# Scores of two heads, then the part of an expert, then the scores of the other two heads

## The chip, the cores and the metric

The kernel runs on one core of a Trainium2 chip. The metric is the device time of one execution in microseconds (us), as a median over runs. The core has five engines that work from their own instruction queues and meet through semaphores: TensorE (PE in the profile, its weight loads PEld), VectorE (DVE), ScalarE (ACT), GpSimd (POOL) and SyncE (SP, which issues most transfers). SBUF is the working memory. PSUM, with eight banks of 128 x 512 f32, is where TensorE writes.

## The reference, cut to what matters

One layer over 2048 tokens of 128 features. First an attention with 16 heads of 8 features, in which a sigmoid stands where a softmax would be; then a mixture of experts: each token goes to two of eight experts, and a shared expert sees every token.

```python
align = jnp.einsum('bhtd,bhsd->bhts', q, k)
resonance = jax.nn.sigmoid((align - THRESH) * SHARP)
modulation = resonance * gate_q[..., :, None] * gate_k[..., None, :]
collapse = jnp.einsum('bhts,bhsd->bhtd', modulation, v)
...
out = out + comb[:, e:e + 1] * _swiglu(xn, gate_up_w[e], down_w[e])   # for the two experts of a token
out = out + _swiglu(xn, shared_gate_up_w, shared_down_w)
```

## The kernel before

The tokens are cut into four blocks of 512 (`TB`). Attention of block `i` is done in 64 rounds `k` (`ROUNDS`): four groups of four heads (`g = k // 16`), and for each group 16 tiles of 128 keys (`s = k % 16`). In a round TensorE computes the scores of four heads against one key tile (`scores`), ACT puts the sigmoid over them (`sigmoids`), and TensorE multiplies the result by the gated values and adds it up in the bank `AV` (`values`). `values` runs one round late: round `k` does the scores of `k` and the values of `k - 1`.

The scores of a round are two halves of two heads. A head has 32 contracted rows, head `j` of the group on partitions `32 j` to `32 j + 31`, so its matmul uses a quarter of the array's rows, and the four matmuls of a round use four different quarters. A half goes to a pair of PSUM banks, and one ACTIVATE of 128 x 1024 takes it. There are three such pairs (`S[0:2]`, `S[2:4]`, `UO`), used in turn: half `n` may be written when the sigmoid of half `n - 3` is done (`scores_before`). With two halves a round, the first half of round `k` waits for the second sigmoid of round `k - 2`, and the second half for the first sigmoid of round `k - 1`. After each half a semaphore (`score_mm`) tells ACT.

The experts of the block before are computed in the gaps of the same rounds. `NT` = 15 tiles of 128 rows sorted by expert, and the shared expert, make 16 units `u`. Each unit has three kinds of part: part 0 is the gate projection (`gate`, 12 matmuls, for the shared expert 3), part 2 the up projection (`up`, as many), and part 1 the down projection of unit `u - 3` (`hidden_out`, 12 matmuls) with the turning of a tile (`turn_tile`, 2 matmuls). All parts, and the projections of the attention, share one bank (`GB`). So each waits for the engine that reads what was there before (the list `readers`): mostly DVE, which clips the gate, multiplies gate by up, or copies the output. Which round has which part is fixed by `parts_in`: rounds 22 to 60 have one each, rounds 17, 20 and 21 have the shared expert's, and in blocks 2 and 3 rounds 10 and 12 to 19 carry the last nine parts of the block before. Rounds of `i` = 0 have no parts, and behind round 63 of `i` = 3 comes a last stage without attention. Within the three blocks, `i` = 1 has 42 rounds with a part, `i` = 2 and 3 have 50 each: 142 together.

The order on TensorE in a round is written out by hand in `rounds`: the scores, the steps of the routing (`project_last`, `turn_tokens`, `route`, `rank`, only in rounds 1, 8, 9 and 11), the first part, the values of the round before, and then whatever else the round has (a second part, `gate_rows`). Steps of the end of a block (`finish`) run on DVE in rounds 36 to 41 of blocks 2 and 3.

Of the kernel before, what the change touches and what calls it, by code (L numbers as in the profile page):

```python
# [27 lines left out]
G = 4  # L28
# [72 lines left out]
def scores_before(n):  # L101

    return max([m + 1 for m in range(max(n - 40, 0), n) if score_pair(m) == score_pair(n)], default=0)
# [6 lines left out]
def parts_in(i, k):  # L110

    parts = [(i - 1, *CARRIED_PARTS[n])
             for n, at in enumerate(CARRIED) if at == k and i > 1]
    parts += [(i, 0, part) for part, at in SHARED_PARTS.items() if at == k]
    if FIRST_PART <= k <= LAST_PART:
        parts.append((i, *PARTS[k - FIRST_PART]))
    return parts if i > 0 else []


def build(nc, x, wqkv, vecs, consts, ident16, wo, router, gu, down, out):  # L120
    ctx = ExitStack()
    with ctx:  # L122
# [110 lines left out]
        heads = [m[:, :, 0:2 * D].rearrange("p s (n d) -> p s n d", d=HD) for m in raw]  # L233
# [119 lines left out]
        def turned_with(u):  # L353

            return (0, 1) if u == 0 else tuple(range(u + 1, min(u + 2, NT)))
# [12 lines left out]
        def score_banks(i, k, half):  # L368

            pair = score_pair(2 * (i * ROUNDS + k) + half)  # L370
            return UO[:] if pair == 2 else S[:, 2 * pair:2 * pair + 2, :]
# [44 lines left out]
        def wait(eng, s, value):  # L416

            if not isinstance(value, int) or value > 0:
                eng.wait_ge(s, value)
# [323 lines left out]
        def _(pe):  # L743
# [48 lines left out]
                                split[:, n // 2, first:first + G, :, :].rearrange("p n s d -> p (n s d)"), id16[:, K_IDENT:K_IDENT + P])  # L792
                    mm.then_inc(qk_tr, 1)

            def scores(i, k):
                g, s = k // ST, k % ST
                if i == 0:
                    pe.wait_ge(qk_copied, 4 * (s // SUB + 1))
                elif s == 0:
                    pe.wait_ge(q_staged[g], i * 16)  # L800
                for j in range(G):
                    if j % 2 == 0:

                        wait(pe, sig_done, scores_before(2 * (i * ROUNDS + k) + j // 2))
                        if (i, k, j) == (0, WIDE_FROM, 0):

                            pe.wait_ge(qk_copied, 4 * NB)
                        banks = score_banks(i, k, j // 2)
                    r = slice(32 * j, 32 * j + 32)
                    mm = nc.tensor.matmul(banks[:, j % 2, :], kT[r, g, s * P:(s + 1) * P], qT[r, g, :], start=True, stop=True)  # L810
                    if j % 2 == 1:
                        mm.then_inc(score_mm, 1)
# [35 lines left out]
            def project_last(i):  # L848

                pe.wait_ge(coll_ready, i * NG)  # L850
                for j in range(SUB):
                    mm = nc.tensor.matmul(GB[:, j * D:(j + 1) * D], coll[:, NG - 1, j * P:(j + 1) * P], wo_sb[:, NG - 1, :],
                                          start=False, stop=j == SUB - 1)
                mm.then_inc(proj_mm, 1)

            def turn_tokens(i):
                pe.wait_ge(n2_ready, i)
                for j in range(SUB):
                    mm = nc.tensor.transpose(GB[:, j * P:(j + 1) * P], tok[:, j, :], ident)
                mm.then_inc(n2_mm, 1)  # L860

            def route(i):

                pe.wait_ge(xn_ready, i * 3 - 2)
                for j in range(SUB):
                    mm = nc.tensor.matmul(GB[:, j * E:(j + 1) * E], xnT[:, j * P:(j + 1) * P], rws[:], start=True, stop=True)
                mm.then_inc(router_mm, 1)
# [6 lines left out]
            def rank(i, readers):  # L874

                free(readers)
                pe.wait_ge(mask_ready, i)
                under, ones = id16[:, K_UNDER:K_UNDER + P], id16[:, K_ONES:K_ONES + P]
                for j in range(SUB):
                    for m in range(j + 1):  # L880
                        nc.tensor.matmul(GB[:, j * E:(j + 1) * E], under if m == j else ones, mask[:, m, :], start=m == 0, stop=m == j)
                for m in range(SUB):
                    mm = nc.tensor.matmul(GB[:, SUB * E:(SUB + 1) * E], ones, mask[:, m, :], start=m == 0, stop=m == SUB - 1)
                mm.then_inc(rank_mm, 1)
# [28 lines left out]
            def gate(i, u, readers):  # L913

                n, m = (i - 1) * NU + u, (i - 1) * NT + u - 1
                free(readers)
                if u == 0:
                    pe.wait_ge(xn_ready, i * 3)
                    pe.wait_ge(weights_split, E + 1)
                else:  # L920
                    pe.wait_ge(tile_turned, m + 1)
                    pe.wait_ge(gu_loaded[m % GS], (m // GS + 1) * 16)
                expand(gate_bank(i, u), u, m, 0).then_inc(gate_mm, 1)
                return [(gate_clipped, n + 1)]

            def up(i, u, readers):

                n, m = (i - 1) * NU + u, (i - 1) * NT + u - 1
                free(readers)
                expand(up_bank(i, u), u, m, 1).then_inc(up_mm, 1)  # L930
                return [(prod_ready, n + 1)]
# [13 lines left out]
            def hidden_out(i, u, readers):  # L945

                n, m = (i - 1) * NU + u, (i - 1) * NT + u - 1
                free(readers)
                pe.wait_ge(hid_split, n + 1)
                pe.wait_ge(dn_loaded[m % DS], (m // DS + 1) * 16)  # L950
                w = dn_ring[:, m % DS, :].rearrange("p (h c d) -> p h c d", h=2, c=FC)
                for c in range(FC):
                    t = slice(c * P, (c + 1) * P)
                    mm = three_passes(y_bank(i, u), hid_hi[:, n % LAG, t], hid_lo[:, n % LAG, t], w[:, 0, c, :], w[:, 1, c, :],
                                      c == 0, c == FC - 1)
                mm.then_inc(down_mm, 1)
                return [(y_ready, n + 1)]

            def turn_tiles(i, u, readers):

                free(readers)
                for t in turned_with(u):
                    turn_tile(i, t)
                return [(tile_turned, (i - 1) * NT + turned_until(u))]

            def unit_part(i, u, part, readers):

                if part == 0:
                    return gate(i, u, readers)
                if part == 2:  # L970
                    return up(i, u, readers)
                read = []
                if u > LAG:
                    read += hidden_out(i, u - LAG, readers)
                if turned_with(u):
                    read += turn_tiles(i, u, [] if u > LAG else readers)
                return read

            def rounds(i, experts, first=0):

                readers = [(gateb_copied, i * NG)] if experts else [(qk_copied, 4 * NB)]
                for k in range(first, ROUNDS):
                    parts = parts_in(i, k)
                    scores(i, k)
                    if experts:
                        if k == OUT_ROUND:
                            project_last(i)
                        if k == TURN_ROUND:
                            turn_tokens(i)
                        if k == ROUTE_ROUND:  # L990
                            route(i)
                            readers = [(diff_ready, i)]
                        if k == RANK_ROUND:
                            rank(i, readers)
                            readers = [(slot_ready, i)]
                    for j, u, part in parts[:1]:
                        readers = unit_part(j, u, part, readers)
                    if PROJECT_ROUND <= k < PROJECT_ROUND + NG - 1:

                        project_first(i, k - PROJECT_ROUND, readers)  # L1000
                    if k > 0:
                        values(i, k - 1)
                    elif i > 0:
                        values(i - 1, ROUNDS - 1)
                    if (i, LAG, 1) in parts:
                        readers = shared_out(i, readers)
                    for j, u, part in parts[1:]:
                        readers = unit_part(j, u, part, readers)
                    if k in GATE_ROUNDS:
                        g = GATE_ROUNDS.index(k)  # L1010
                        gate_rows(i, g, readers)
                        readers = [(gateb_copied, i * NG + g + 1)]
# [567 lines left out]
```

## Time and profile before

| | us |
|---|---|
| median of 3 runs | 731.08 (730.95 to 734.54) |
| the profiled execution: its time | 732.92 |
| the profiled execution: its span, first to last instruction | 730.2 |
| TensorE busy | 619.7 (85%) |
| ACT busy | 563.5 (77%) |
| DVE busy | 418.6 (57%) |
| POOL busy | 164.6 (23%) |
| mean granted clock of TensorE | 0.94 of full speed |

The rounds of `i` = 0 to 3 run from about 37 to 607 us; `i` = 1 begins at 183.84, `i` = 2 at 319.11, `i` = 3 at 463.72. The busy time of a matmul is taken to a modelled end, so consecutive matmuls overlap in the rows; what a step costs on TensorE is read from start to start. L810 is the matmul of the scores, L824 that of the values, L898 that of a part, L697 the sigmoid of the scores on ACT, L672 the sigmoid of a gate.

### The profile page before, as it was taken

How to read it: one execution, taken by the hardware profiler on the slowest of the kernel's cores; microseconds unless marked ns; L12 is line 12 of the kernel's file. 1: busy time of each engine (PE TensorE's matmuls, PEld its weight loads, DVE VectorE, ACT ScalarE, POOL GpSimd, SP SyncE). 2: the span in 40 equal slices, each digit the busy share in tenths (PEclk: the TensorE clock that was granted, in tenths of full speed). 3: DMA queues.
4: the chain of work that ended last, by engine and by line, in shares of the span. 5: the costliest groups of instructions: out<-in, count | busy, mean ns of one | idle time of the engine just before them, and what ended most of it. 6: DMA issues, size and time to landing. Idle time of an engine off the chain costs nothing. (4 is left out here: it accounts for less than half of the span.)

```text
span 730.2 us, 15309 instructions
## 1 busy us (share of the span) xinstructions
PE 619.7 (85%) x5928; PEld 259.5 (36%) x5928; DVE 418.6 (57%) x1107; ACT 563.5 (77%) x661; POOL 164.6 (23%) x149
## 2 busy tenths in 40 slices
PE   3587999999999999998999899989998994368840
PEld 2452211112223344432334344333343442347730
DVE  6775184920653555447545855475458554648984
ACT  1579799999999899988898899888988993005520
POOL 1122000000041221100543121014431220237642
PEclk9998999999999999999999999999999998559975
DMA  8600001620044344400643354005444440158921
GB/s 325 226 30 30 30 9 19 264 104 1 9 137 128 123 142 120 142 26 6 181 151 119 122 137 143 23 23 164 144 114 120 146 138 4 40 148 267 319 69 51
DMA packets 47639, 82.02 MB, mean 112 GB/s; under 512 B 5456, under 2 KB 25168, under 8 KB 47568
## 3 DMA queue, kind: packets, MB, share of 16 engines
q1 hardware_dynamic: 45088, 76.31, 32.8%
q0 software_dynamic: 2048, 4.20, 1.9%
q8 instruction: 47, 0.77, 0.4%
q10 hardware_dynamic: 432, 0.54, 0.3%
q14 instruction: 24, 0.20, 0.1%
HBM read 64.59 MB, written 16.45 MB: 111 GB/s over the span
## 5 line engine op out<-in xcount | busy, mean ns | idle before, releaser
L697 ACT ACTIVATE res<-S 128x1024 f32<-128x1024 f32 x348 | 349.2, 1067 | 22.5 <-PE S L810 11.9
L824 PE MATMUL AV<-res,vg 128*8 128x512 f32 x2048 | 305.4, 599 | 1.5 <-DVE coll L1199 1.5
L697 ACT ACTIVATE res<-UO 128x1024 f32<-128x1024 f32 x164 | 175.2, 1069 | 10.6 <-PE S L810 9.7
L600 POOL TENSOR_TENSOR work<-work 128x512 f32<-128x512 f32 x64 | 81.8, 1279 | 243.9 <-DVE work L1320 243.0
L810 PE MATMUL S<-qT,kT 32*128 32x512 f16 x696 | 104.5, 387 | 2.7 <-ACT res L697 2.4
L898 PE MATMUL GB<-xT,gu_ring 128*128 128x128 f16 x1164 | 84.2, 224 | 11.1 <-DVE slot L1300 3.9
L672 ACT ACTIVATE work<-work,scl 128x512 f32<-128x512 f32 x64 | 46.8, 731 | 57.8 <-DVE work L1313 57.7
L574 POOL DMA_INDIRECT xs_dram<-xrow,slot x32 | 32.1, 1002 | 243.1 <-DVE slot L1300 235.1
L898 PEld LDWEIGHTS GB<-xT,gu_ring 128*128 128x128 f16 x1164 | 67.5, 100 | 32.6 <-issue 17.4
L810 PEld LDWEIGHTS S<-qT,kT 32*128 32x128 f16 x696 | 25.9, 91 | 146.6 <-ACT res L697 93.2
L1313 DVE TENSOR_SCALAR work<-GB,scl 128x512 f32<-128x512 f32 x56 | 45.3, 809 | 52.3 <-PE GB L898 52.1
L810 PE MATMUL UO<-qT,kT 32*128 32x512 f16 x328 | 63.6, 384 | 0.4 <-ACT res L697 0.3
L824 PEld LDWEIGHTS AV<-res,vg 128*8 128x8 f32 x2048 | 36.4, 87 | 71.1 <-ACT res L697 30.3
L1320 DVE SCALAR_TENSOR_TENSOR work<-work,scl,GB 128x512 f32<-128x512 f32 x48 | 35.8, 746 | 37.8 <-PE GB L898 37.8
L1332 DVE TENSOR_TENSOR hid_lo<-work,hid_hi 128x512 f16<-128x512 f32 x64 | 52.2, 816 | 3.2 <-ACT hid_hi L687 1.6
L898 PE MATMUL GB<-dn_ring,hid_hi 128*128 128x128 f16 x360 | 38.8, 232 | 14.9 <-DVE work L1313 7.1
L810 PEld LDWEIGHTS UO<-qT,kT 32*128 32x128 f16 x328 | 15.4, 90 | 69.4 <-ACT res L697 47.3
L1471 DVE TENSOR_SCALAR gate_q<-GB 128x512 f32<-128x512 f32 x16 | 11.0, 690 | 50.2 <-PE GB L835 50.0
L1340 DVE COPY xT<-GB 128x256 f16<-128x256 f16 x45 | 12.9, 291 | 44.1 <-PE GB L893 43.9
L898 PEld LDWEIGHTS GB<-dn_ring,hid_hi 128*128 128x128 f16 x360 | 27.8, 103 | 26.1 <-issue 10.7
L898 PE MATMUL GB<-dn_ring,hid_lo 128*128 128x128 f16 x180 | 35.7, 232 | 0.0
L1199 DVE TENSOR_TENSOR coll<-AV,gate_q 128x512 f32<-128x512 f32 x16 | 11.0, 690 | 36.8 <-PE AV L824 36.8
(232 smaller groups left out, 662.1 us busy)
## 6 DMA issues: line engine op xcount, KB each, us to landing
gu_ring<-gu_dram SPq DMA_DIRECT2D x60, 512.0 KB, 3.4
dn_ring<-dn_dram SPq DMA_DIRECT2D x60, 256.0 KB, 2.9
work<-in_gu SPq DMA_DIRECT2D x8, 512.0 KB, 10.4
gu_dram<-gu_ring SPq DMA_DIRECT2D x8, 512.0 KB, 2.6
ys_dram<-work SPq DMA_DIRECT2D x60, 64.0 KB
work<-in_down SPq DMA_DIRECT2D x8, 256.0 KB, 11.1
dn_dram<-dn_ring SPq DMA_DIRECT2D x8, 256.0 KB, 2.9
work<-xs_dram SPq DMA_DIRECT2D x4, 448.0 KB, 4.7
```

The lines of the kernel that those rows point to most:

```text
L574: nc.gpsimd.indirect_dma_start(xs_dram, bass.IndirectOffsetOnAxis(ap=slot[:, i % 2, n:n + 1], axis=0), xrow[:, n % SUB, :], None).then_inc ...
L600: nc.gpsimd.tensor_tensor(hid[u % 2], prod[u % 2], sg[u % 2], ALU.mult).then_inc(hid_ready, 1)
L672: nc.scalar.activation(sg[c % 2], gate_c[c % 2], ACT.Sigmoid, scale=scale(S_SIG)).then_inc(sg_ready, 1)
L697: nc.scalar.activation(res[:, k % 2, 2 * half:2 * half + 2, :].rearrange("p h t -> p (h t)"), score_banks(i, k, half).rearrange("p h t -> ...
L810: mm = nc.tensor.matmul(banks[:, j % 2, :], kT[r, g, s * P:(s + 1) * P], qT[r, g, :], start=True, stop=True)
L824: mm = nc.tensor.matmul(AV[32 * j:32 * j + HD, :], vg[:, s, G * g + j, :], res[:, k % 2, j, :], start=s == 0, stop=s == ST - 1)
L898: mm = nc.tensor.matmul(bank, w, v, start=first and n == 0, stop=last and n == 2)
L1199: v.tensor_tensor(coll[:, g, :], AV[:], gate_q[:], ALU.mult).then_inc(coll_ready, 1)
L1313: v.tensor_scalar(gate_c[u % 2], gate_bank(i, u), scale(S_HI), scale(S_LO), ALU.min, ALU.max).then_inc(gate_clipped, 1)
L1320: v.scalar_tensor_tensor(out=prod[u % 2], in0=gate_c[u % 2], scalar=scale(S_PROD), in1=up_bank(i, u), op0=ALU.mult, op1=ALU.mult).then_inc ...
L1332: v.tensor_tensor(hid_lo[:, n % LAG], hid[u % 2], hid_hi[:, n % LAG], ALU.subtract).then_inc(hid_split, 1)
L1340: v.tensor_copy(xT[:, t % 3, :], tile_bank(i, t)).then_inc(tile_turned, 1)
```

## The change

`scores` takes the heads as an argument. In a round with a part, TensorE first gets the scores of heads 0 and 1, then the steps that stood between scores and values, the part among them, then the scores of heads 2 and 3, then the values. In rounds without a part all is as before. No instruction is added or taken away other than the repeated waits at the head of `scores`.

```diff
-            def scores(i, k):
+            def scores(i, k, heads=range(G)):
                 g, s = k // ST, k % ST
                 if i == 0:
                     pe.wait_ge(qk_copied, 4 * (s // SUB + 1))
                 elif s == 0:
                     pe.wait_ge(q_staged[g], i * 16)
-                for j in range(G):
+                for j in heads:
                     if j % 2 == 0:
...
                     parts = parts_in(i, k)
-                    scores(i, k)
+                    scores(i, k, (0, 1) if parts else range(G))
                     if experts:
...
                     for j, u, part in parts[:1]:
                         readers = unit_part(j, u, part, readers)
+                        scores(i, k, (2, 3))
                     if PROJECT_ROUND <= k < PROJECT_ROUND + NG - 1:
```

## Rows read from the trace of the kernel before

**Rows 1.** Page, part 1: busy us (share of the span) x instructions.

```profile
PE 619.7 (85%) x5928; PEld 259.5 (36%) x5928; DVE 418.6 (57%) x1107; ACT 563.5 (77%) x661; POOL 164.6 (23%) x149
```

**Rows 2.** Windows: stretches with parts of blocks 1 (two) and 2 (three).

```profile
core 0: us, PE busy (x) PEld busy (x) DVE busy (x) ACT busy (x) POOL busy (x), PEclk, DMA share, GB/s
215.55:237.94 22.39, 22.02 (x199) 6.51 (x197) 7.47 (x13) 22.39 (x27) 5.47 (x6) 1.00 0.50 160
237.94:311.41 73.47, 71.80 (x824) 30.92 (x822) 37.45 (x70) 69.13 (x78) 14.51 (x12) 1.00 0.44 132
338.25:363.97 25.72, 22.32 (x252) 9.07 (x250) 17.97 (x49) 21.10 (x26) 11.01 (x10) 1.00 0.41 125
363.97:387.00 23.03, 22.32 (x233) 8.04 (x230) 9.59 (x17) 22.41 (x26) 7.75 (x8) 1.00 0.43 132
387.00:456.02 69.02, 65.49 (x750) 28.14 (x747) 42.27 (x96) 62.61 (x70) 17.17 (x15) 1.00 0.46 137
```

**Rows 3.** Timeline of PE, rounds 34 and 35: start, us, what [idle before <-releaser].

```profile
394.71 0.39 PE L810 MATMUL S<-qT,kT 32*128 32x512 f16 x4
395.04 0.84 PE L898 MATMUL GB<-xT,gu_ring 128*128 128x128 f16 x12
395.81 1.05 PE L824 MATMUL AV<-res,vg 128*8 128x512 f32 x8
396.79 0.39 PE L810 MATMUL UO<-qT,kT 32*128 32x512 f16 x2
...
398.00 1.04 PE L824 MATMUL AV<-res,vg 128*8 128x512 f32 x8
398.98 0.39 PE L810 MATMUL S<-qT,kT 32*128 32x512 f16 x2
```

**Rows 4.** Timeline of PE, rounds 24 and 27: halves that start apart.

```profile
371.25 0.39 PE L810 MATMUL S<-qT,kT 32*128 32x512 f16 x2
371.80 0.39 PE L810 MATMUL UO<-qT,kT 32*128 32x512 f16 x2 [0.15 <-ACT res L697]
372.12 0.84 PE L898 MATMUL GB<-xT,gu_ring 128*128 128x128 f16 x12
...
377.47 0.39 PE L810 MATMUL S<-qT,kT 32*128 32x512 f16 x2
377.89 0.39 PE L810 MATMUL UO<-qT,kT 32*128 32x512 f16 x2
378.21 0.84 PE L898 MATMUL GB<-xT,gu_ring 128*128 128x128 f16 x12
```

**Rows 5.** Timeline of PE, end of round 31: gate rows, then scores.

```profile
389.08 0.39 PE L834 MATMUL GB<-qT,gm_a 128*128 128x512 f16 x1
389.31 0.38 PE L835 MATMUL GB<-qT,gm_b 128*128 128x512 f16 x1
389.62 0.39 PE L810 MATMUL UO<-qT,kT 32*128 32x512 f16 x2
```

**Rows 6.** Timeline of ACT in rounds 34 and 35.

```profile
395.14 1.94 ACT L697 ACTIVATE res<-S 128x1024 f32<-128x1024 f32 x2 [0.43 <-PE S L810]
396.96 0.72 ACT L672 ACTIVATE work<-work,scl 128x512 f32<-128x512 f32 x1
397.58 1.02 ACT L697 ACTIVATE res<-UO 128x1024 f32<-128x1024 f32 x1
```

**Rows 7.** Timeline of PE: rounds 11, 19, 33, 38, 40, 41 of block 2, which waited.

```profile
341.86 0.41 PE L881 MATMUL GB<-mask,id 128*128 128x8 f16 x10 [1.13 <-DVE work L1313]
...
362.23 0.27 PE L898 MATMUL GB<-dn_ring,hid_hi 128*128 128x128 f16 x2 [0.24 <-issue]
...
393.73 1.04 PE L824 MATMUL AV<-res,vg 128*8 128x512 f32 x8 [0.23 <-DVE coll L1199]
...
403.90 0.28 PE L898 MATMUL GB<-dn_ring,hid_hi 128*128 128x128 f16 x2 [0.37 <-DVE work L1313]
...
408.59 0.84 PE L898 MATMUL GB<-xT,gu_ring 128*128 128x128 f16 x12 [0.36 <-DVE work L1320]
...
412.39 0.28 PE L898 MATMUL GB<-dn_ring,hid_hi 128*128 128x128 f16 x2 [1.65 <-DVE work L1313]
```

## The prediction

> **What bounds the kernel now.** The page first: TensorE is busy for 85% of the span and ACT for 77%, so either may set the pace, and the average doesn't tell where [rows 1]. Next I cut the rounds with parts into stretches [rows 2]. In three of the five TensorE is the busier engine, by 2.7 us in 73.5, 1.2 in 25.7 and 2.9 in 69.0; in the two short ones that hold the first rounds of a block's new parts, ACT is (22.39 against 22.02 us, and 22.41 against 22.32). In the two stretches that last longest, about 70 us each with a part in every round, ACT has idle time left. The granted clock is 1.00 throughout, which is the 2.4 GHz level.
>
> Then the order of time on TensorE in two such rounds [rows 3]. The reader should look at the starts. Scores at 394.71, part at 395.04, values at 395.81, next scores at 396.79: 0.33, 0.77 and 0.98 us, together 2.08, and every step begins as soon as the one before it lets it. No step is marked with a wait. The next round, with a down projection and a turned tile, takes 2.19 in the same way (396.79 to 398.98). So TensorE's own work in line sets the length of these rounds: three rounds (gate, down, up) take 2.08 + 2.19 + 2.08 = 6.35 us. ACT beside it: two sigmoids take 1.82 us from start to start (395.14 to 396.96) and a gate's sigmoid 0.62 (396.96 to 397.58) [rows 6], which makes 6 x 0.91 + 0.62 = 6.08 us in three rounds. ACT waits 0.43 us for the scores there. TensorE is the bound, with little to spare under it.
>
> **The change part by part.** Nothing is removed. Each of the 142 rounds with a part issues its four score matmuls and four weight loads as before; two of each move behind the part. What is lost is that the four run side by side. All four start within a hundredth of a us and the part follows 0.33 after them [rows 3]. What would two cost alone? The trace has such a case. In rounds 24 and 27 the second half had to wait for ACT and started 0.55 and 0.42 us behind the first; from its start to the part it took 0.32 both times (371.80 to 372.12, 377.89 to 378.21) [rows 4]. So two heads take as long as four. The first half keeps the 0.32 before the part, and the second adds 0.32 between part and values, on the engine that sets the pace. 142 x 0.32 = 45.4 us.
>
> Bounds of that price: a matmul of 512 columns that follows another over the whole array starts 0.23 behind it (389.08 to 389.31), while the step from the last of them to the scores takes 0.31 (389.31 to 389.62) [rows 5]. So about 0.1 us belongs to the change of kind between two steps, and the new order has one more such change in a round. I keep 0.32, since the case of rows 4 is the very pair of matmuls; the low end is 0.23 a round (142 x 0.23 = 32.7 us) and the high end the row's own 0.39 (55.4 us). The Trainium skill says why the order should matter (TensorEngine Tiling (Array Packing), Key Properties): changing the tiling mode drains the engine, and going from quarter-row matmuls to a full-array part and back is such a change. The trace agrees, with 0.31 to 0.33 where the kind changes against 0.23 where it doesn't. By the figure of TensorE: Matmul & The Clock Gate, Back-to-back issue gap, which has no drain in it (about 216 ns for 512 columns), the sum would be an estimate of 142 x 0.216 = 30.7 us before give-backs.
>
> What the longer rounds give back, because a wait shrinks:
> - The second half's own wait for ACT in rounds 24 and 27 falls under the part: 0.55 + 0.42 = 0.97 us in each of three blocks [rows 4]. The other rounds of the stretch from 387 have no such wait.
> - In blocks 2 and 3, waits for DVE that stand in a later round, where DVE's own chain doesn't move. An idle time in the row counts from a modelled end, which is some 0.07 behind the earliest next start (0.39 against 0.32). The 1.13 us of round 11 take in the whole 0.32 that round 10 is longer. Rounds 19, 33, 38 and 40 lose 0.24, 0.23, 0.37 and 0.36, each with its 0.07: 1.48. Of the 1.65 in round 41 I count 1.0 as the pairs of three rounds, 39 to 41, which stand between the up projection that starts DVE's chain and this part [rows 7]. Together 0.32 + 1.48 + 1.0 = 2.8 us a block.
> - In block 1 only round 33 repeats (0.3). In its first stretch ACT is never idle [rows 2], and two rounds without a part (18 and 19) let it go on while round 17 is longer: about 0.5, an estimate.
>
> By block: the first 42 x 0.32 - 0.97 - 0.3 - 0.5 = 11.7; second and third 50 x 0.32 - 0.97 - 2.8 = 12.2 each. Sum **36.1 us**. The profiled execution took 732.92; it would take 769.0. The median of the runs stands 1.84 below it, so I predict 731.08 + 36.1, about **767 us**.
>
> What else moves. Behind the pair stand the values of the round before; they need the second sigmoid of that round, which now starts later. From the late half's start to the values that read it there are 0.32 + 0.98 + 0.32 + 0.77 + 0.32 = 2.7 us; ACT answers 0.43 behind a score and takes 0.91 to 1.02, so 1.45. In a round without a part that follows (11, 18, 61) it is 0.32 + 0.98 + 0.32 = 1.62, still enough. ACT then idles more, and that costs nothing: its 6.08 us stand against 7.31 in three rounds. SP waits for the last scores of a group before it loads the queries of the next block, and gets that signal about a part later, 0.8 us; the data are needed some 50 rounds on. The weight loads of SP wait for the ends of the parts, which come later but with more time to the next use. No wait on POOL moves except with the round. The repeated wait for the queries is long met. The stage behind the last round isn't touched.
>
> **The rivals.**
> - **The waits don't shrink.** The price is right, but DVE, POOL and ACT chains stretch along with the rounds, because each starts from a matmul of a part. For it: many of the waits are for DVE work that such a matmul released. Against: the DVE time between has the same length as before. 731.08 + 45.4 = 776.5.
> - **A cheap pair.** The added step costs only its stream, 0.23 [rows 5], if the change of kind hides under the values' start. Against: both lone pairs took 0.32. 731.08 + 32.7 - 9.3 = 754.5.
> - **Not slower: the pair runs beside the part.** The two late heads use half the rows; if they could stream while the last matmuls of the part still do, they would add nothing, and the 3 x 0.97 us of waits would be gained: 728.2, within half a per cent of before. It decides if the added step is under about 0.02 us a round (2.9 / 142). Against it: after scores the part never starts earlier than 0.32, and from a part to the next step the rows show 0.77 for 12 matmuls, nothing overlapped.
> - **ACT becomes the bound.** Scores come one half at a time, so each sigmoid might have to pay its start: 0.43 + 1.02 = 1.45. Two a round and a third of 0.62 make 3.1 us against 2.1 now, 142 x 1.0: some 870 us. It holds only if halves are waited for in turn; the three pairs of banks leave one half ready ahead, and 2.7 us stand against 1.45. Chance small.
>
> **How the numbers follow.** Forecast 0.80; waits that don't shrink 0.09; cheap pair 0.06; pair beside the part 0.03; ACT 0.02. The range runs from the cheap pair to the dear one: 754 to 777 (0.39 a round less the give-backs is 55.4 - 9.3 = 46.1, or 777). Half a per cent, 3.7 us, is about what a measurement of this kernel can tell. Slower by more than that: 0.96; within it 0.03; faster 0.01.
>
> **What would show it.** In the timeline of TensorE, a round like round 34 should read: two scores, 0.32 later the part, 0.77 later two scores, 0.32 later the values, 0.98 to the next round; 2.40 in place of 2.08, and 2.51 for the down projection. Rounds without a part stay as they are. The waits of rows 7 for DVE in rounds 19, 33, 38 and 40 should be gone and that of round 41 smaller; those in rounds 12, 16, 18, 32 and 48, where the part waits for something that the step just before it released, should stay. ACT should show idle time in nearly every round with a part, and TensorE no wait for ACT at the values. I am wrong if the round grows by much less than 0.32, if a lone pair in front of the values costs another time than one in front of a part, or if the values begin to wait for sigmoids.

## The result, and the profile after

The changed kernel takes 770.47 us (766.85 to 770.82), the kernel before beside it 731.02: a ratio of 1.0534, with a 95% interval of 1.0511 to 1.0558. It is slower by 39.4 us. The forecast was 767 us, 36.1 us more, in a range of 754 to 777. The profiled execution took 770.63 us with a span of 768.6, against 732.92 and 730.2.

The page's part 1 of the changed kernel: busy us, share of the span, instructions.

```profile
PE 661.7 (86%) x5928; PEld 270.9 (35%) x5928; DVE 419.2 (55%) x1107; ACT 579.0 (75%) x661; POOL 164.0 (21%) x149
```

TensorE issues the same 5928 matmuls and is busy for 42.0 us more [rows 1]. The other engines have the work they had. ACT's 15 us more are not work. Two lines of the page's part 5, changed kernel:

```profile
L697 ACT ACTIVATE res<-S 128x1024 f32<-128x1024 f32 x348 | 353.0, 1061 | 41.0 <-PE S L810 32.5
L824 PE MATMUL AV<-res,vg 128*8 128x512 f32 x2048 | 306.1, 601 | 0.9 <-DVE coll L1200 0.9
```

A sigmoid takes 1061 ns on the mean, against 1067 before. But the records of two sigmoids in a row overlap by some 0.1 us, and where ACT idles between them they no longer do: its idle time before this line is 41.0 us, against 22.5 before.

The windows view of the changed kernel, cut at the same rounds as [rows 2]: length, busy time and instructions of each engine, granted clock, DMA.

```profile
215.56:239.53 23.97, 23.79 (x198) 7.02 (x195) 7.47 (x13) 23.36 (x27) 5.78 (x6) 1.00 0.47 155
239.53:323.08 83.55, 82.09 (x824) 33.80 (x821) 37.64 (x70) 72.93 (x78) 14.51 (x12) 1.00 0.39 116
349.93:380.52 30.59, 27.49 (x251) 10.82 (x248) 17.99 (x49) 22.01 (x26) 10.55 (x10) 0.89 0.34 109
380.52:406.06 25.54, 25.01 (x233) 8.84 (x230) 9.59 (x17) 23.15 (x26) 8.06 (x8) 1.00 0.38 116
406.06:482.83 76.77, 74.70 (x750) 30.75 (x747) 42.56 (x96) 66.39 (x71) 17.15 (x15) 1.00 0.41 122
```

Each stretch grew: by 1.58, 10.08, 4.87, 2.51 and 7.75 us. The prediction's terms, 0.32 for each round with a part less the waits that shrink there, come to 1.41, 10.3, 2.25, 2.55 and 7.43. Only the third is off by more than 0.4, and it is the one whose granted clock isn't 1.00. TensorE is now the busier engine in all five.

The timeline of TensorE in the changed kernel, round 24 and round 34 of block 2, each to the start of the next; it answers to [rows 3, 4].

```profile
389.06 0.39 PE L810 MATMUL S<-qT,kT 32*128 32x512 f16 x2
389.38 0.84 PE L898 MATMUL GB<-xT,gu_ring 128*128 128x128 f16 x12
390.16 0.39 PE L810 MATMUL UO<-qT,kT 32*128 32x512 f16 x2
390.48 1.04 PE L824 MATMUL AV<-res,vg 128*8 128x512 f32 x8
391.45 0.39 PE L810 MATMUL S<-qT,kT 32*128 32x512 f16 x2
...
414.42 0.39 PE L810 MATMUL S<-qT,kT 32*128 32x512 f16 x2
414.74 0.84 PE L898 MATMUL GB<-xT,gu_ring 128*128 128x128 f16 x12
415.52 0.39 PE L810 MATMUL S<-qT,kT 32*128 32x512 f16 x2
415.83 1.04 PE L824 MATMUL AV<-res,vg 128*8 128x512 f32 x8
416.81 0.39 PE L810 MATMUL UO<-qT,kT 32*128 32x512 f16 x2
```

Round 34 reads 0.32, 0.78, 0.31, 0.98: four steps in place of three, 2.39 us in place of 2.08. A pair costs 0.32 in front of the part and 0.31 behind it. Round 24, whose second half had waited for ACT until 0.55 behind the first, now has no wait and takes 2.39 in place of 2.62.

ACT in rounds 34 and 35 of the changed kernel; compare [rows 6].

```profile
414.85 2.12 ACT L697 ACTIVATE res<-S 128x1024 f32<-128x1024 f32 x2 [0.27 <-PE S L810]
416.87 0.71 ACT L672 ACTIVATE work<-work,scl 128x512 f32<-128x512 f32 x1
417.48 1.01 ACT L697 ACTIVATE res<-UO 128x1024 f32<-128x1024 f32 x1
418.45 1.02 ACT L697 ACTIVATE res<-S 128x1024 f32<-128x1024 f32 x1
```

Two sigmoids now take 2.02 from start to start rather than 1.82, since the second waits for its late scores. Of the 123 rounds 20 to 60 of the three blocks, ACT now idles for more than 0.05 us in 115; before it was 44. It delays nobody: the values' line of the page above (L824) has 0.9 us of idle time in all, and DVE ended it.

### The profile page after: what moved, and what is told of

The parts are those of the page before. It is cut to its first block and busy times, and to the rows that moved or that the text cites. A ratio compares the mean times of both kernels' runs of the same rounds, so it can differ in the third digit from the quotient of the medians.

```text
span 768.6 us, 15317 instructions
## 1 busy us (share of the span) xinstructions
PE 661.7 (86%) x5928; PEld 270.9 (35%) x5928; DVE 419.2 (55%) x1107; ACT 579.0 (75%) x661; POOL 164.0 (21%) x149
## 5 line engine op out<-in xcount | busy, mean ns | idle before, releaser
L697 ACT ACTIVATE res<-S 128x1024 f32<-128x1024 f32 x348 | 353.0, 1061 | 41.0 <-PE S L810 32.5
L824 PE MATMUL AV<-res,vg 128*8 128x512 f32 x2048 | 306.1, 601 | 0.9 <-DVE coll L1200 0.9
L810 PE MATMUL S<-qT,kT 32*128 32x512 f16 x696 | 122.5, 389 | 2.3 <-ACT res L697 2.1
L810 PEld LDWEIGHTS S<-qT,kT 32*128 32x128 f16 x696 | 29.8, 91 | 156.8 <-issue 93.7
L824 PEld LDWEIGHTS AV<-res,vg 128*8 128x8 f32 x2048 | 36.4, 87 | 86.7 <-issue 52.8
L898 PE MATMUL GB<-dn_ring,hid_hi 128*128 128x128 f16 x360 | 39.4, 234 | 13.2 <-DVE work L1314 5.4
```

The source lines that it names most:

```text
L697: nc.scalar.activation(res[:, k % 2, 2 * half:2 * half + 2, :].rearrange("p h t -> p (h t)"), score_banks(i, k, half).rearrange("p h t -> ...
L824: mm = nc.tensor.matmul(AV[32 * j:32 * j + HD, :], vg[:, s, G * g + j, :], res[:, k % 2, j, :], start=s == 0, stop=s == ST - 1)
L898: mm = nc.tensor.matmul(bank, w, v, start=first and n == 0, stop=last and n == 2)
```

## The experiments

The question was what the 0.32 us are made of and whether the lateness of the second half has a share in it. In what follows a step is a run of matmuls of one kind on TensorE: the scores (32 rows each), a part (the full array) or the values (four tiles of 8 columns). A change of kind is the passage from one step to the next. All kernels do the full computation in another order; the second cuts two matmuls in two, and the third does two of them twice.

**The part first.** All four scores behind the part, side by side.

```diff
                     parts = parts_in(i, k)
-                    scores(i, k)
+                    if not parts:
+                        scores(i, k)
...
                         readers = unit_part(j, u, part, readers)
+                        scores(i, k)
```

> The part stands before all four scores in the 142 rounds; the four run side by side again, and all of them come later than in the changed kernel. If the price is the added step (two heads take as long on TensorE as four), none is added here: 733 to 740 us, the few us above 731 because in the rounds where the part waits for DVE (12, 16, 18, 30, 32, 41, 48) 0.32 us of scores no longer lie under the wait. If the price is that scores reach ACT late, it is as large here or larger: 765 to 785.

Measured 746.18 us, 1.0197 (1.0151 to 1.0243). Later scores than in the changed kernel, and yet 24 us less than it: no extra step, no such price. But it missed its own estimate by 6 us. In its profiled execution 1.8 us of that is a low granted clock in rounds 12 and 13 of block 2, of which more below. The rest lies with the values. In rounds 22 to 30, where ACT is busiest, they take up to 1.54 (376.54 to 378.08) in place of 0.98. From 34 on most rounds take what they took before, and the values in every third one are stretched, as in the timeline of TensorE in rounds 35 and 36 of block 2:

```profile
405.77 0.39 PE L810 MATMUL UO<-qT,kT 32*128 32x512 f16 x2
...
408.17 1.29 PE L824 MATMUL AV<-res,vg 128*8 128x512 f32 x8
409.40 0.84 PE L898 MATMUL GB<-xT,gu_ring 128*128 128x128 f16 x12
```

And ACT of the same kernel in the same rounds:

```profile
405.83 0.72 ACT L672 ACTIVATE work<-work,scl 128x512 f32<-128x512 f32 x1
406.44 1.02 ACT L697 ACTIVATE res<-UO 128x1024 f32<-128x1024 f32 x1
407.35 1.96 ACT L697 ACTIVATE res<-S 128x1024 f32<-128x1024 f32 x2
```

The scores of 405.77 find a gate's sigmoid in front of them on ACT. Their own run from 406.44 and 407.35, the second until about 408.4, and the values that read them are up at 408.17. They take 1.23 in place of 0.98. So a late half does cost something where a gate's sigmoid stands in front of it on ACT and 2.4 us lie between the scores and their values. In the two rounds out of three there that have no such sigmoid in front nothing is stretched.

**Sixteen columns.** A change of kind on TensorE with hardly any stream: the last 16 columns of heads 2 and 3 behind the part, and ACT told only then.

```diff
+                    c = slice(TB - 16, TB) if rest else slice(0, TB - 16 if rest is False and j > 1 else TB)
-                    mm = nc.tensor.matmul(banks[:, j % 2, :], kT[r, g, s * P:(s + 1) * P], qT[r, g, :], start=True, stop=True)
+                    mm = nc.tensor.matmul(banks[:, j % 2, c], kT[r, g, s * P:(s + 1) * P], qT[r, g, c], start=True, stop=True)
...
                         readers = unit_part(j, u, part, readers)
+                        scores(i, k, True)
```

> Scores as in the kernel before, but of heads 2 and 3 the last 16 of 512 columns are computed behind the part, with their own weight loads; the second half is told to ACT only then. An extra change of kind on TensorE with nearly no streaming. If 0.32 is a stream of 0.21 plus 0.11 for the change of kind, this costs about 0.11 a round: 142 x 0.11 = 15.6, less some 5 of shrunk waits: 738 to 745 us. If the change of kind is free: 731. If the whole 0.32 belongs to it, or to the late half: 765 to 770.

Measured 742.91 us, 1.0160 (1.0123 to 1.0197), in the range expected for 0.11 a round. The timeline of TensorE in one round:

```profile
399.52 0.39 PE L811 MATMUL S<-qT,kT 32*128 32x512 f16 x4
399.84 0.84 PE L899 MATMUL GB<-xT,gu_ring 128*128 128x128 f16 x12
400.62 0.18 PE L811 MATMUL S<-qT,kT 32*128 32x16 f16 x2
400.73 1.04 PE L825 MATMUL AV<-res,vg 128*8 128x512 f32 x8
```

The small pair takes 0.11 (400.62 to 400.73), the scores before the part 0.32 and the part 0.78. ACT gets its second half about 1.2 us behind the first scores of the round (1.4 in the changed kernel), and that adds nothing to the 0.11. Whether the 0.11 is the change of kind itself or another fixed cost of a further step, its weight loads for one, this run doesn't separate.

**The pair twice.** A stream with no change of kind: heads 2 and 3 done twice in a row in front of the part.

```diff
-                for j in range(G):
+                for n, j in enumerate((0, 1, 2, 3, 2, 3) if twice else range(G)):
...
-                    if j % 2 == 1:
+                    if j % 2 == 1 and not (twice and n == 3):
                         mm.then_inc(score_mm, 1)
```

> Before the part, as in the kernel before, but in the 142 rounds the matmuls of heads 2 and 3 are done twice in a row with the same result: the stream of a pair is added and no change of kind. By the added step: about 0.22 a round, 31 us less 6 to 9 of shrunk waits: 753 to 757 us. If the price were only the change of kind: 731 to 735.

Measured 749.53 us, 1.0259 (1.0221 to 1.0297); some 4 us less than expected. The timeline of TensorE:

```profile
402.93 0.61 PE L810 MATMUL S<-qT,kT 32*128 32x512 f16 x6
403.47 0.84 PE L898 MATMUL GB<-xT,gu_ring 128*128 128x128 f16 x12
404.24 1.05 PE L824 MATMUL AV<-res,vg 128*8 128x512 f32 x8
405.22 0.39 PE L810 MATMUL UO<-qT,kT 32*128 32x512 f16 x2
```

Scores to part takes 0.54, 0.22 more. Together with the 0.11 that makes 0.33, the 0.31 to 0.32 of the changed kernel's step. The sum came out lower because this pair stands ahead of the part: in rounds 12, 16, 18, 30, 32, 41 and 48, where the part waits for DVE, it lies under the wait and the round is as long as before. I hadn't counted those.

**The rounds with a gate alone.** The change in 44 of the 142 rounds.

```diff
-                    scores(i, k, (0, 1) if parts else range(G))
+                    scores(i, k, (0, 1) if parts and parts[0][2] == 0 else range(G))
```

> The change in the 44 rounds alone whose first part is a gate (14, 15 and 15 in the three blocks). If each round pays its own step: 44 x 0.32 = 14.1 us, less 2 to 5 for waits: 740 to 744 us. If it is an effect that needs every round (ACT falling behind over a row of rounds), clearly less: 731 to 735.

Measured 739.17 us, 1.0118 (1.0080 to 1.0155): 8.5 us more than before beside it, a little under the range. The rounds with a gate are 0.31 longer and the others unchanged, except that waits in rounds 11, 24, 27, 38 and 41 shrink. Each round pays for itself.

**Three heads, then one.**

```diff
-                    scores(i, k, (0, 1) if parts else range(G))
+                    scores(i, k, (0, 1, 2) if parts else range(G))
...
-                        scores(i, k, (2, 3))
+                        scores(i, k, (3,))
```

> Three heads before the part and one behind it, in place of two and two. If a step costs the same for one head as for four, the time is that of the changed kernel, 766 to 771 us. If the price goes with the matmuls that move, half of it: about 750.

Measured 768.09 us, 1.0508 (1.0467 to 1.0550), the time of the changed kernel. The timeline of TensorE, one round:

```profile
416.19 0.39 PE L810 MATMUL S<-qT,kT 32*128 32x512 f16 x2
416.20 0.38 PE L810 MATMUL UO<-qT,kT 32*128 32x512 f16 x1
416.52 0.84 PE L898 MATMUL GB<-xT,gu_ring 128*128 128x128 f16 x12
417.29 0.39 PE L810 MATMUL UO<-qT,kT 32*128 32x512 f16 x1
417.61 1.04 PE L824 MATMUL AV<-res,vg 128*8 128x512 f32 x8
```

One head behind the part takes 0.32 (417.29 to 417.61), and three in front of it 0.33 (416.19 to 416.52). The price is of the step, not of the matmuls in it.

**Halves of neighbouring rounds together.** The late half moves behind the values, beside the first half of the next round: the pairs are side by side again, with one step a round.

```diff
                     for j, u, part in parts[:1]:
                         readers = unit_part(j, u, part, readers)
-                        scores(i, k, (2, 3))
+                        if not together:
+                            scores(i, k, (2, 3))
...
+                    if together:
+                        scores(i, k, (2, 3))
+                        scores(i, k + 1, (0, 1))
+                        ahead = k + 1
```

> Between two rounds that both have a part, the late half is put behind the values, next to the first half of the following round: four heads side by side again, one step a round, but the half is only one part ahead of the values that read it. If the number of steps were all: 731 to 736 us. If the answer of ACT counts too (0.43 to the start of a sigmoid and 0.97 for it, 1.4 us, against 0.32 + 0.77 = 1.09 until the values come), the values wait some 0.35 a round: 770 to 790, with TensorE idle at the values and waiting for ACT, and ACT with little idle time.

Measured 773.47 us, 1.0587 (1.0545 to 1.0628). The timeline of TensorE, one round:

```profile
415.33 0.39 PE L810 MATMUL UO<-qT,kT 32*128 32x512 f16 x2
...
415.66 0.84 PE L898 MATMUL GB<-xT,gu_ring 128*128 128x128 f16 x12
416.43 1.44 PE L824 MATMUL AV<-res,vg 128*8 128x512 f32 x8
417.80 0.39 PE L810 MATMUL S<-qT,kT 32*128 32x512 f16 x2
```

And ACT:

```profile
415.76 1.02 ACT L697 ACTIVATE res<-UO 128x1024 f32<-128x1024 f32 x1 [0.53 <-PE S L810]
```

Four scores take 0.33 to the part again, so no step is added; but the values need 1.37 in place of 0.98. The values begin at 416.43, 1.10 behind the scores of the late half, and the sigmoid of that half runs until 416.78. So two heads' values start at 416.43 and the other two, which read the late half, at 416.84 by the trace; from there it takes 0.96 more. Here lateness costs 0.39 in most rounds. In the changed kernel 2.7 us lie between, and it costs nothing.

**Rounds 24 and 27 alone.**

```diff
-                    scores(i, k, (0, 1) if parts else range(G))
+                    scores(i, k, (0, 1) if parts and k in (24, 27) else range(G))
```

> The change in rounds 24 and 27 alone (6 rounds in all), the ones in which the second half waited for ACT by 0.55 and 0.42 us. In the changed kernel these rounds got shorter, by 0.23 and 0.10. If the pair lies under that wait: 730 to 731 us, up to 1.0 us less than before, nothing if ACT sets the pace of that stretch anyway. If the step is paid there too: 6 x 0.32 = 1.9 more, 733.

Measured 729.19 us against 730.17, 0.9980 (0.9958 to 1.0001): no difference that the runs can tell. In the trace round 24 of block 2 is 0.21 shorter (371.11 to 373.52, [rows 4] 2.62), but from the values of round 7 to those of round 63 the block gains only 0.1. ACT, which is busy for 22.41 of the 23.03 us of that stretch before [rows 2], shows no idle time in this run either from 369.04 to 385.40, so it sets the pace there.

## Why the prediction was right

**What bounds.** TensorE's line of work did set the length of the rounds with a part. Nearly all of them grew by 0.31 or 0.32, the others being those in which a wait shrank, round 17 of block 1, where ACT has no idle time, and rounds 12 and 13 with a low clock, and no round without a part grew. Block 1, at a granted clock of 1.00 in both profiles, is the clean test: from the values of round 1 to those of round 63 it went from 131.02 to 142.67 us, 11.65 more; the prediction had 11.7.

**The price of the pair.** 0.32 from the lone halves of [rows 4] held, in front of the part and in front of the values. The experiments split it into 0.21 to 0.22 of stream and 0.11 for the further step. The cheap pair at 0.23, a rival of the prediction, is thereby out: the cost of the step beyond its stream isn't hidden. So is the pair beside the part. The Trainium skill's rule that a change of the tiling mode drains the engine (TensorEngine Tiling (Array Packing), Key Properties) agrees with the 0.11 us that 16 columns cost; no run here shows the drain by itself.

**What the waits give back.** These are waits of TensorE after the change, in the timeline of the changed kernel; they answer to [rows 7].

```profile
353.53 0.41 PE L881 MATMUL GB<-mask,id 128*128 128x8 f16 x10 [0.82 <-DVE work L1314]
...
356.56 0.39 PE L898 MATMUL GB<-dn_ring,hid_hi 128*128 128x128 f16 x2 [1.23 <-DVE slot L1301]
...
425.31 0.39 PE L810 MATMUL S<-qT,kT 32*128 32x512 f16 x2
...
432.92 0.29 PE L898 MATMUL GB<-dn_ring,hid_hi 128*128 128x128 f16 x2 [1.14 <-DVE work L1314]
```

Round 11 waits 0.31 less, as foreseen, and in rounds 19, 33, 38 and 40 no wait is left. The rival by which waits don't shrink fell. In round 41 I was wrong: 1.65 became 1.14, which gives back 0.51 and not 1.0. DVE's chain there begins with the turned tile of round 38 and not with the up projection of round 39. From the end of part 38 to the start of part 41 it takes 7.61 us in both kernels (425.31 to 432.92; before 404.78 to 412.39). DVE's first and last instruction of that chain, changed kernel, then before:

```profile
425.47 0.29 DVE L1341 COPY xT<-GB 128x256 f16<-128x256 f16 x1 [0.24 <-DVE work L1450]
...
432.05 0.81 DVE L1314 TENSOR_SCALAR work<-GB,scl 128x512 f32<-128x512 f32 x1
```

```profile
404.94 0.29 DVE L1340 COPY xT<-GB 128x256 f16<-128x256 f16 x1
...
411.52 0.81 DVE L1313 TENSOR_SCALAR work<-GB,scl 128x512 f32<-128x512 f32 x1
```

They stand 6.58 us apart both times, with DVE busy between. The three longer rounds shorten the waits inside by 0.96 in all, and 0.43 of it I had already counted in round 40.

**ACT.** The last rival, ACT as the bound, didn't come: a sigmoid answers 0.43 behind its score, and there were 2.7 us to do it in. The experiment with neighbouring halves shows where this rival would have begun.

**The missing 3 us.** The rounds of the profiled execution sum to 39.5 us more, not 36.1. Of the difference, 1.0 is round 41 in two blocks, and 2.9 is the granted clock in rounds 12 and 13, for which the prediction had no term. Against them, the added step was 0.314 on the mean in rounds that wait for nothing (42 to 60 without 48), not 0.32, which takes back 0.9 over 142 rounds; smaller terms make the rest. That this offsets the mistake in round 41 is luck. The windows view of rounds 12 and 13 in block 2, changed kernel:

```profile
354.94:360.32 5.38, 4.15 (x28) 1.51 (x25) 4.31 (x15) 3.05 (x4) 2.93 (x3) 0.57 0.26 78
360.32:363.69 3.37, 3.37 (x29) 1.52 (x26) 0.75 (x1) 1.89 (x2) 1.55 (x3) 0.67 0.68 230
```

The same two rounds of block 2 with three heads, then one:

```profile
354.94:358.62 3.68, 2.70 (x27) 1.10 (x27) 3.40 (x13) 2.61 (x4) 1.99 (x2) 1.00 0.11 35
358.62:361.01 2.39, 2.39 (x26) 0.98 (x25) 1.26 (x2) 2.05 (x3) 1.78 (x3) 1.00 0.95 311
```

and round 12 of block 3 in the kernel before:

```profile
487.89:492.51 4.62, 3.64 (x28) 1.50 (x25) 4.28 (x15) 2.94 (x4) 2.17 (x3) 0.63 0.18 57
```

At the 2.4 GHz level rounds 12 and 13 take 3.68 and 2.39; in block 2 of the changed kernel they took 5.38 and 3.37, for the most part at 1.2 GHz: 2.7 us. In block 3 both kernels lost, the changed one 1.49 and the one before 1.25 (4.62 against 3.37 in its block 2). Without this the rounds grew by 39.5 - 2.7 - 0.24 = 36.6 us. The last stage, which neither touches, was 1.1 us shorter in this execution (121.9 against 123.0), also at a slightly higher clock (0.73 against 0.71).

What stays open is whether the change makes the low clock in round 12 likelier. The kernel with three heads and one kept 1.00 in both blocks in its profiled execution, but its wait isn't quite the same. Its part of round 12 in block 2:

```profile
356.11 0.29 PE L898 MATMUL GB<-dn_ring,hid_hi 128*128 128x128 f16 x2 [0.98 <-DVE slot L1301]
```

The changed kernel's stands further up, at 356.56: 1.23 us idle, since nothing runs between the first two scores and the part. With three heads the third starts 0.25 us later, as the second half did before (0.99 idle). The nine profiled kernels make 18 passes of round 12 in blocks 2 and 3. The clock fell during this wait or just behind it in all six passes that waited 1.23 to 1.55 us (the changed kernel, the part first, the neighbouring halves), and in two of the twelve that waited 0.77 to 0.99 (block 3 of the kernel before and of the sixteen columns). So the change may well bring part of this loss with it; but that is one profile of each kernel, and a cause isn't shown.

## What to carry to other kernels

Small matmuls that use different quarters of the array cost one step together: 0.32 us for one, two, three or four of them here. Whoever separates them pays the step again, 142 times in this kernel, where TensorE sets the pace. Ask first which engine has idle time in the round: a split that gives TensorE something to do while it waits for ACT is worth nothing where it doesn't wait. And when a shrunk wait is counted, follow the other engine's chain to its start, or the same gain is counted twice.

## What the runs showed of the hardware

- A further step of two quarter-row matmuls between full-array ones and the values costs 0.11 us with nearly no columns to stream (16); a further pair of 512 columns beside its like, without a change of kind, costs 0.22.
- One head of 32 rows takes as long as two, three or four side by side: 0.31 to 0.33 us from its start to the next step.
- In or just behind the wait of round 12, which follows another in round 11 (1.23 and 0.82 us in the changed kernel), the granted clock fell to 1.2 GHz in 8 of 18 profiled passes: in all six of the kernels whose round 12 waited 1.23 to 1.55 us, and in two of the twelve that waited 0.77 to 0.99. In the changed kernel and the one before it cost 1.25 to 2.7 us where it fell, part of it in round 13, which had no wait.
